# Two-layer transformer in one kernel: the query and key stacks' parts get memory of their own, head loads bring 24 or 25 rows, and the first front is reordered

## The reference, cut to what matters

```python
x = x + _L0_attn_ref(_layernorm(x), Wqkv, Wo)    # rotary position code, softmax over 1024 keys
x = x + _L0_ffn_ref(_layernorm(x), ...)          # shared expert + 7 routed ones, top 2
x = x + _L1_attn_ref(_layernorm(x), ...)         # layernorm with gamma and beta, biases
x = x + _L1_ffn_ref(_layernorm(x), ...)          # attention with relative positions, then 32 experts, top 4

# in _L0_attn_ref
q = q * cos + rotate_half(q) * sin
k = k * cos + rotate_half(k) * sin
scores = jnp.einsum('bqhd,bkhd->bhqk', q, k) * scale
attn = jax.nn.softmax(scores, axis=-1)
out = jnp.einsum('bhqk,bkhd->bqhd', attn, v)
```

## Time and profile before

| what | us |
|---|---|
| median of 3 runs | 2066.3 (2059.05 to 2070.08) |
| profiled execution, its own time | 2062.49 |
| its span in the trace | 2060.5 |
| PE busy | 1918.0 (93%) |
| DVE busy | 1382.8 (67%) |
| ACT busy | 1205.9 (59%) |
| POOL busy | 507.2 (25%) |
| DMA moved | 198.58 MB, mean 96 GB/s |

### The profile page before, as it was taken

The page is one execution under the profiler, slowest core; times in us unless marked ns, Lnnn a source line. Parts: engine busy times, 40 slices in busy tenths (PEclk is TensorE's granted clock), DMA queues, the critical chain, the costliest instruction groups (busy, mean ns, idle before and its releaser), DMA issues.

```text
span 2060.5 us, 40384 instructions
## 1 busy us (share of the span) xinstructions
PE 1918.0 (93%) x13792; PEld 1159.1 (56%) x13792; DVE 1382.8 (67%) x1778; ACT 1205.9 (59%) x2289; POOL 507.2 (25%) x493
## 2 busy tenths in 40 slices
PE   5999999799985999999689999999999999977998
PEld 2333333577762333333356666666666666665887
DVE  6999997556658899996565455555555555346776
ACT  2699999466652799999224444444444444433553
POOL 2000000178862100000222222222222222103654
PEclk8799999899996799999799999999999999988999
DMA  8444542121106445453512211111112211014554
GB/s 275 135 129 127 129 128 77 60 88 63 52 0 196 113 119 134 123 136 86 170 52 60 58 48 50 47 48 47 47 51 61 51 50 47 8 33 179 213 218 144
DMA packets 90189, 198.58 MB, mean 96 GB/s; under 512 B 19872, under 2 KB 49312, under 8 KB 84768
## 3 DMA queue, kind: packets, MB, share of 16 engines
q1 hardware_dynamic: 90080, 197.10, 32.5%
HBM read 162.42 MB, written 36.18 MB: 96 GB/s over the span
## 4 chain that ended last, share of the span: by engine, by line
PE 46%; DVE 2%; DMA 1%; SPq 1%; issue 0%; ACT 0%; DVEq 0%
PE PS L749 17%; PE PS L833 8%; PE PS L761 6%; PE PS L735 6%; PE PS L744 4%; PE PS L724 4%; DVE M L1233 1%; SPq L369 1%; DMA Ks<-in_kv 0%; DMA Ws_r<-w_stack 0%; PE PS L768 0%; PE PS L575 0%; PE PS L707 0%; PE PS L566 0%; PE PS L545 0%
## 5 line engine op out<-in xcount | busy, mean ns | idle before, releaser
L1212 DVE TENSOR_REDUCE M<-PS 128x1 f32<-128x1024 f32 x512 | 595.1, 1217 | 23.0 <-PE PS L630 17.6
L1486 ACT ACTIVATE PR<-PS 128x512 f32<-128x512 f32 x1024 | 539.2, 602 | 41.7 <-PE PS L645 21.3
L1522 ACT ACTIVATE PR<-PS 128x512 f32<-128x512 f32 x512 | 305.8, 598 | 378.5 <-PE PS L749 374.7
L1233 DVE TENSOR_REDUCE M<-PS 128x1 f32<-128x1024 f32 x256 | 311.8, 1221 | 218.4 <-PE PS L735 211.3
L655 PE MATMUL PS<-PR,Va 128*32 128x256 f32 x4096 | 332.2, 397 | 15.6 <-POOL Va L1669 2.7
L645 PE MATMUL PS<-Qs_r,Ks_r 32*128 32x512 f32 x1024 | 310.6, 508 | 0.5 <-ACT PR L1486 0.4
L630 PE MATMUL PS<-Ks_r,Qs_r 32*128 32x512 f32 x1024 | 269.6, 524 | 23.0 <-DVE M L1212 10.3
L630 PEld LDWEIGHTS PS<-Ks_r,Qs_r 32*128 32x128 f32 x1024 | 99.6, 192 | 228.4 <-issue 153.2
L1228 DVE TENSOR_TENSOR rt<-PS,rel 128x512 f32<-128x512 f32 x128 | 88.4, 691 | 162.5 <-PE PS L707 160.9
L655 PEld LDWEIGHTS PS<-PR,Va 128*32 128x32 f32 x4096 | 83.5, 108 | 149.7 <-ACT PR L1486 62.0
L1669 POOL TENSOR_TENSOR Va<-Vt,nil 128x64 f32<-128x64 f32 x96 | 27.8, 293 | 536.7 <-PE PS L655 533.3
(11 more groups left out here) (204 smaller groups left out, 3034.8 us busy)
## 6 DMA issues: line engine op xcount, KB each, us to landing
Qs_r<-q_stack SPq DMA_DIRECT2D x384, 128.0 KB, 2.6
Ks_r<-k_stack SPq DMA_DIRECT2D x384, 128.0 KB, 3.1
Qs<-g_dram SPq DMA_DIRECT2D x29, 1024.0 KB, 4.7
o_dram<-Ob SPq DMA_DIRECT2D x96, 128.0 KB, 2.0
Ks<-g_dram SPq DMA_DIRECT2D x10, 1024.0 KB, 4.8
q_stack<-hl_r SPq DMA_DIRECT2D x18, 256.0 KB, 3.3
k_stack<-hl_r SPq DMA_DIRECT2D x18, 256.0 KB, 4.1
q_stack<-PR_r SPq DMA_DIRECT2D x18, 256.0 KB, 3.2
```

Source lines behind the costliest of these rows:

```text
L1212: e.tensor_reduce(M[:, s, qt:qt + 1], PS[:, 2 + 2 * (qt % 2):4 + 2 * (qt % 2), :] .rearrange("p a b -> p (a b)"), AX.X, ALU.max, negate=Tr ...
L1233: e.tensor_reduce(M[:, s, qt:qt + 1], PS[:, bk:bk + 2, :].rearrange("p a b -> p (a b)"), AX.X, ALU.max, negate=True).then_inc(max_done, 1)
L1486: e.activation(PR[:, kt % 4, qh * GW:(qh + 1) * GW], bank(RING[(x + turn) % 3]), ACT.Exp, scale=SCALE).then_inc(exp_done, 1)
L1522: e.activation(PR[:, kt % 4, qh * GW:(qh + 1) * GW], bank(TURN[kt % 2][qh]), ACT.Exp)\
```

## The change

Five things change.

1. The parts of the stacks in front(0) get memory of their own for each group (in BIG, which lies idle there), in front(2) for groups 2 and 3. ACT's waits for stores before it writes them go or are loosened. ACT's wait for all stores at the start of attention(0) and attention(1) goes too; SP now waits for them itself, behind the first maximum rows (`stored`).
2. The three pad DMAs move into experts0, and the seven loads of constants to the end of attention(0). One small DMA stays at the start, for the row of ones of `k_stack`.
3. Head loads in attention(0) and attention(1) bring 24 rows of q and 25 of k in place of 32, and PE's products read 24 or 25 rows. The relative attention still loads 32.
4. In front(0) and front(2) heads 0 and 1 are both loaded ahead of the stores of group 2, and head 2 ahead of those of group 3.
5. In front(0) PE turns the next group between this group's k and q products, ACT copies xT ahead of the parts of the group before, and the two rotary additions move from DVE to POOL.

```diff
+        wide = BIG_r[:].rearrange("p (g a b t) -> p g a b t", g=NG, a=2, b=2)
+        HL = {0: [wide[:, g] for g in range(NG)],
+              2: [hl0_r, wide[:, 2], wide[:, 3], hl0_r],
+              3: [PAIR[g % 2] for g in range(NG)]}
...
-            def load_qk(n, s):
-                for to, of in ((Qs_r, q_stack), (Ks_r, k_stack)):
+            def load_qk(n, s, q_depth=MROW, k_depth=MROW + 1):
+                for to, of, depth in ((Qs_r, q_stack, q_depth), (Ks_r, k_stack, k_depth)):
                     for r in range(4):
-                        e.dma_start(to[r * KR:(r + 1) * KR, s, :].bitcast(F32), of[bass.ds(n, 1)].rearrange("n r t -> (n r) t"))\
-                            .then_inc(qk_in[s], 16)
+                        e.dma_start(to[r * KR:r * KR + depth, s, :].bitcast(F32),
+                                    of[bass.ds(n, 1), 0:depth, :].rearrange("n r t -> (n r) t")).then_inc(qk_in[s], 16)
...
                 max_rows(0, 0)
+                if a < 2:
+                    stored(2 * (a + 1))
                 load(3, 3)
...
                 position(NH - 3, 1, False)
+                if a == 0:
+                    constants()
...
-                            load_qk(0, 0)
+                            e.wait_ge(one_in, 16)
+                            load_qk(0, 0)
+                            load_qk(1, 1)
+                    if g == 3 and f < 3:
+                        load_qk(2, 2)
                     q_out(a, g)
                     k_out(a, g)
...
(PE, front)
                         for w, bk in ((2, 3), (3, 4), (0, 1), (1, 2)):
+                            if f == 0 and w == 2:
+                                e.wait_ge(krot_ok, g)
+                            if f == 0 and w == 0:
+                                if g + 1 < NG:
+                                    turn_rows(g + 1)
+                                e.wait_ge(qrot_ok, g)
...
(ACT, attention)
-                e.wait_ge(c_in, 16 * N_CONST)
-                stacks_stored(a)
+                if a == 0:
+                    e.wait_ge(split_k, NG)
+                    e.wait_ge(split_q, NG)
...
(POOL, front(0), each group)
+                        e.wait_ge(krot_ok, g + 1)
...
+                        e.tensor_tensor(kin[g % 2], rt[:, 0, :], rt[:, 1, :], ALU.add).then_inc(kin_ok, 1)
+                        e.wait_ge(qrot_ok, g + 1)
...
+                        e.tensor_tensor(qk[:, 0, :], rtq[:, 0, :], rtq[:, 1, :], ALU.add).then_inc(qin_ok, 1)
```

More of the change, by code:

```diff
@@ L319, in _, with constants, pads @@
             e.dma_start(rope[:], A["rope"]).then_inc(rope_in, 16)
[L320 to L327, removed]
+            def constants():
+                loads = [(w_out[:], A["w_out"]), (cols[:], A["cols"]), (rows[:], A["rows"]),
+                         (w_rt0[:], A["w_rt0"]), (w_rt1[:], A["w_rt1"]),
+                         (w_qkv[:, 1:3, :], A["w_qkv"][:, 1:3, :]), (rel[:], A["rel"][:, 1:3, :])]
+                for dst, src in loads:
+                    e.dma_start(dst, src).then_inc(c_in, 16)
+                assert len(loads) == N_CONST
+            def pads():
+                for d, src, w in ((q_stack, 0, L), (k_stack, 1, L), (w_stack, 0, 2 * P)):
+                    e.dma_start(d[:, MROW:KR, :], A["pad"][src:src + 1, :, 0:w].broadcast_to([NH, KR - MROW, w]))\
+                        .then_inc(pad_in, 16)
+            e.dma_start(k_stack[:, MROW:MROW + 1, :], A["pad"][1:2, 0:1, 0:L].broadcast_to([NH, 1, L])).then_inc(one_in, 16)
             def q_out(a, g):
@@ L481, in front @@
                     if g == 2:
[L483 to L486, removed]
+                        stored(2 * a + 1)
                         if f == 3:
+                            e.wait_ge(pad_in, 16 * 3)
                             e.wait_ge(w_out_ok, 16 * 6)
@@ L490, in front @@
                         else:
+                            e.wait_ge(one_in, 16)
                             load_qk(0, 0)
+                            load_qk(1, 1)
+                    if g == 3 and f < 3:
+                        load_qk(2, 2)
                     q_out(a, g)
                     k_out(a, g)
-                    if g == 2:
+                    if g == 2 and f == 3:
                         for n in range(1, 3):
[L496 to L503, removed]
+                            load_rel(n, n)
+                if f == 3:
+                    stored(2 * (QKV.index(f) + 1))
             def attention1():
@@ L577, in spread, with turn_rows @@
                     m.then_inc(spread_ok, 1)
+                def turn_rows(g):
+                    e.wait_ge(xn_ok, 4 * f + g + 1)
+                    if a2 is None:
+                        e.wait_ge(xh_ok, 4 * (f // 4) + g)
+                    if f == 0:
+                        e.wait_ge(xs_ok, g)
+                    for t in range(GT):
+                        m = transpose(PS[:, 0, t * P:(t + 1) * P], xn[:, t, :])
+                    m.then_inc(xT_ok, 1)
+                if f == 1:
+                    e.wait_ge(c_in, 16 * N_CONST)
                 if a is not None:
@@ L589, in front @@
                         spread(3)
[L590 to L595, removed]
+                    if f > 0 or g == 0:
+                        turn_rows(g)
                     if g:
@@ L1397, in projected @@
                     else:
                         e.wait_ge(proj_ok, pr + 1)
-                        e.wait_ge(stk_out[half], 16 * TERMS * (2 * a2 + g // 2))
+                        if f == 3:
+                            e.wait_ge(stk_out[half], 16 * TERMS * (2 * a2 + g // 2))
+                        elif g == 3:
+                            e.wait_ge(stk_out[0], 16 * TERMS * (2 * a2 + 1))
                         if f == 2:
-                            e.activation(hls[g % 2][:, 1, 0, :], bank(3), ACT.Identity, bias=cols[:, 3:4]).then_inc(khi_ok, 1)
+                            e.activation(HL[f][g][:, 1, 0, :], bank(3), ACT.Identity, bias=cols[:, 3:4]).then_inc(khi_ok, 1)
@@ L1402, in projected @@
                         else:
-                            e.activation(hls[g % 2][:, 1, 0, :], bank(3), ACT.Copy).then_inc(khi_ok, 1)
+                            e.activation(HL[f][g][:, 1, 0, :], bank(3), ACT.Copy).then_inc(khi_ok, 1)
                         e.wait_ge(proj_ok, pr + 2)
-                        e.wait_ge(stq_out[half], 16 * TERMS * (2 * a2 + g // 2))
+                        if f == 3:
+                            e.wait_ge(stq_out[half], 16 * TERMS * (2 * a2 + g // 2))
+                        elif g == 3:
+                            e.wait_ge(stq_out[0], 16 * TERMS * (2 * a2 + 1))
```

76 lines of the change are left out of this document (44 added, 32 removed).

## The result

| | us |
|---|---|
| before, median of 6 runs on the same chip | 2064.14 |
| after, median of 6 runs | 2080.13 (2072.94 to 2102.75) |
| ratio | 1.0091, 95% interval 1.0048 to 1.0134 |
| profiled execution after, its own time | 2072.94 |
| its span | 2071.1 |

The change made the kernel slower by about 16 us. I had forecast 2065.0 and a range up to 2080. The profiled execution is one of the two shortest after; its span is 10.6 us above that of before, and the trace can show only those.

A forecast was written before the change was run, and what follows sets the result against it. DVE was taken to bound the attentions' steady part, so only the two starts counted: −0.4 − 0.9 = −1.3 us from the 2066.3 median gave 2065.0. The range was 2055 to 2080.

The forecast's parts named there:

- Matmuls of 24 or 25 rows for 32: Products in attention(0) and attention(1): a row's time follows its 512 columns (0.50 us), so fewer rows cost 0.
- Front(0): First front: ends at 40.4 us at full PE clock or 45.1 at slow; head 0's loads begin 36.0 or 37.9.
- Loads on fewer engines: Head loads in both attentions: q on 12 DMA engines, k on 5; 5.1 us per head against 3.5 before.
- rival A: Head loads use all 16 engines whatever their rows; both starts reach DVE's bound, 2058 to 2061 us; chance 0.18.
- Starts: position(0) of attention(0) changes by −0.4 us (−3.4 to +7), that of attention(1) by −0.9 us (−3.5 to +5).
- The steady part: Inside attentions a head costs 9.39 us of DVE and PE; smaller loads gain nothing, maximum rows keep 0.65 us in hand.
- Rival B: In the attentions' steady part five engines delay each head's maximum rows; 2083 us at 20 GB/s per engine; chance 0.15.
- Constants: Loads moved to the end of attention(0): cost 0, covered by the last head's work; up to 4 us once if not.
- Rival C: Both starts come out near their slow ends (slow clock, k at 4.9 us): +3 to +10, 2069 to 2076 us; chance 0.12.

The follow-up runs named there:

- b_prod: The kernel before, with score and turned products of attention(0) and attention(1) reading 24 and 25 rows, loads still 32: 2079.31 us, ratio 1.0082.
- b_load: The kernel before, with both head loads and products of 24 and 25 rows in attention(0) and attention(1), nothing else changed: 2078.28 us, ratio 1.0089.
- a_load32: The changed kernel with head loads of 32 rows and pads stored at the start; products still 24 and 25 rows: 2080.72 us, ratio to before 1.0063.
- a_all32: The changed kernel with loads and products of 32 rows, pads at the start, the rest of the change kept: 2059.98 us, ratio to before 0.9983.
- a_act: The changed kernel with loads and products of 32 rows and ACT's constants wait moved to the end of front(1): 2057.36 us, ratio to before 0.9966.
- b_start: The kernel before, with products of 24 and 25 rows only in heads 0 to 5 of each plain attention: 2085.2 us, ratio 1.01.
- b_late: The kernel before, with products of 24 and 25 rows only from head 6 of each plain attention on: 2063.18 us, ratio 0.9994.

## Why the prediction was wrong, step by step

**The step that failed** is "Matmuls of 24 or 25 rows for 32: a row's time follows its 512 columns (0.50 us); I cost 0". The first half held: a matmul takes 0.79 us at 1.2 GHz and 0.50 at 2.4 with 24, 25 or 32 rows. What I left out is that, with fewer rows, the 1.2 GHz last longer after an attention has begun. Its size is about 15 us (b_prod, a ratio of 1.0082). I had named the 0.79 us as the only bound and said that PE's slack would not hide it, and then gave it neither a rival nor a share of the range. None of my three rivals is what happened.

**Front(0)** was right for group 1 with its slow clock: I gave 30.9 us for its low q part, and it came at 31.0, with the clock at 0.52 from 21.0 to 27.6 us. From 27.6 to 44.0 us the clock was at 1.00, and the front's end (ACT's last copy of v) came at 43.1, between the 40.4 of the full clock and the 45.1 of the slow one. Head 0's loads began at 38.4, against 37.9.

**Loads on fewer engines** were right in kind and short in size. Head 0 landed 8.7 us after its first issue, not about 7, and not earlier as rival A (all 16 engines) wanted. The number of engines is right too, by the closing packets that I had read in rows 7: from before to b_load the page's packets under 512 B fall from 19872 to 16032, that is by 3840, and 256 pairs of loads with 12 + 5 in place of 16 + 16 closing packets make 256 × 15 = 3840. In the steady part the DMA share fell from 0.49 to 0.30. The Trainium skill, DMA: Bandwidth & Descriptors, "Why a DMA increments its semaphore by 16 and not by 1", gives the rule that I used, and the later landing with fewer bytes (8.85 against 6.82 us at attention(1)) agrees with it, as do the packets. In time the short loads cost 3 to 4 us at an equal clock, at the two starts, where b_load waits 2.88 us for the maximum rows.

**Starts.** I gave −0.4 and −0.9 us; the trace shows +1.0 and +0.1, both inside their bounds (the upper bound of the first is +6 by its own terms, 37.9 + 31.7 + 0.5 = 70.1 against 64.13, and not +7). That they came near nothing is two terms against each other. In the three changed kernels with loads of 32 rows (a_load32, a_all32, a_act) position(0) of attention(0) began at 62.4, 62.6 and 60.1 us, and attention(1) took 26.5, 28.4 and 27.7 us from head 0's load to its position(0). Against before (64.1 and 28.96) the new order gained 1.5 to 4 and 0.6 to 2.5 us; against the changed kernel (65.1 and 29.09) the short loads took back 2.5 to 5 and 0.7 to 2.6. At attention(0) I expected a wait for the maximum rows. There was none: they were issued at 58.83, and position(0) was bound by DVE, 8.7 us of landing and 18.05 us of score steps. At attention(1) the wait was there, 2.63 us, as I said.

**The steady part** holds a head in 9.39 us as before, and PE waits for no DMA in it. Rival B is refuted.

**Constants** I cost at 0, since their issues had cover. They did: SP issued them at 348 to 352 us, and DVE's wait of 5.2 us behind them lay where the last heads have no scores left to form. But ACT's wait for them, which now stands at the head of front(1), pushed the table load onto the path: 1.3 of the 3.2 us that front(1) lost. The low clock in front(1) was also longer (27.3 us in place of 20.5); how much of the other 1.9 us is from that I did not separate.

**Rival C** (slow ends, "slow clock") priced the low clock in the starts only, through the matmuls before position(0). The clock mattered after it.

What stays open is why fewer rows hold the clock down; the runs show that they do, and where, not how the chip decides. Also open is which of the other parts bring the 4 us of a_all32 beside the gain at the starts; no run splits them. Why b_start lost no less than b_prod, with fewer rows in 12 heads only, is not shown either.

## What to carry to other kernels

Rows of zeros in a matmul may be worth their place: before cutting a product's rows, look in the windows for stretches at half clock in which PE is the bound, and keep the full rows there. Where the clock was at its upper level, in b_late, fewer rows cost nothing. Compare the mean clocks of two kernels before reading a difference of their medians: here the clock hid what the short loads cost. When a wait moves to the head of a stage, look for the table load that stands behind it.

## What the runs showed of the hardware that I had not expected

- TensorE, busy for 42.00 of 42.00 us, stayed at 1.2 GHz throughout (a_load32), and for 45.07 of 45.40 in b_start. The Trainium skill, TensorE: Matmul & The Clock Gate, Part 1, says that the ramp's penalty is under 1% of a typical kernel's span. Here the low stretches at two starts cost 75.1 × 0.33 = 25 us in the kernel before (1.2%) and 143.3 × 0.33 = 47 us in b_start (2.3%), if the price of a step is taken for all of them; the measurement decides.
- The effect is graded by how many of the products have fewer rows: one of the two with 24 or 25 rows 1.0043 and 1.0032, both 1.0082; both with 28 rows 1.0011, not to be told from none.
- With fewer rows the run-to-run spread grew too: 25 us in b_prod (12 runs less its longest), against 12 us in a_all32 (12 runs). It is the spread of the clock: over 143 runs the span follows the time at half clock to within 1.3 us.
